# Local attention's score products: 64x64 tiles of the array, with unseen cells written once a stage

## The reference, cut to what matters

```python
W, H, DH = 64, 8, 64                       # window, heads, width of a head
qkv = x @ Wqkv.T                           # x: layer-normed, 8 x 256 x 128
# q, k, v -> (batch, head, window, 64, 64); ke, ve: the window before, its own, the one after
sim = jnp.einsum('bhnid,bhnjd->bhnij', q, ke) * SCALE
sim = jnp.where(valid[None, None, :, None, :], sim, -1000000000.0)   # no window before the first, after the last
attn = jax.nn.softmax(sim, axis=-1)
o = jnp.einsum('bhnij,bhnjd->bhnid', attn, ve)
...
return o @ Wout.T
```

## Time and profile before

| | us |
|---|---|
| median of three launches | 1091.48 |
| the profiled launch | 1089.49 |
| its span | 1087.7 |
| first routed stage, light branch (about 317 to 503) | 186 |
| second routed stage, light branch (about 800 to 986) | 186 |
| TensorE busy in the span | 966.8 |
| VectorE busy in the span | 670.0 |
| ScalarE busy in the span | 381.5 |

### The profile page before, as it was taken

One profiled execution on the slowest core, in us unless ns is written; L12 is line 12 of the kernel. 1 busy time (PEld: TensorE's weight loads), 2 busy tenths in 40 slices (PEclk: granted clock), 3 DMA queues, 4 the chain that ended last, 5 costly groups with the idle time before them and its releaser, 6 DMA issues.

```text
span 1087.7 us, 23083 instructions
## 1 busy us (share of the span) xinstructions
PE 966.8 (89%) x8840; PEld 698.3 (64%) x8840; DVE 670.0 (62%) x1914; ACT 381.5 (35%) x913; POOL 141.6 (13%) x289
## 2 busy tenths in 40 slices
PE   3499999899559999999999589999879999999997
PEld 3378888788446666667776245555446667667775
DVE  5778787887664565566555456667453665565553
ACT  3321111111333434333332136667623433333332
POOL 5011111110110000000000254350010000000000
PEclk9889898999689999999999569999979999999997
DMA  5000000000000000000000233322000000000000
GB/s 188 0 2 1 2 0 0 0 0 1 0 1 1 1 2 2 2 2 2 1 0 1 60 86 97 82 75 75 3 1 1 2 1 2 2 2 2 10 10 20
DMA packets 13751, 20.07 MB, mean 18 GB/s; under 512 B 1504, under 2 KB 12128, under 8 KB 12256
## 3 DMA queue, kind: packets, MB, share of 16 engines
q1 hardware_dynamic: 13520, 18.67, 5.9%
q10 hardware_dynamic: 144, 0.20, 0.1%
HBM read 14.53 MB, written 4.19 MB: 17 GB/s over the span
## 4 chain that ended last, share of the span: by engine, by line
PE 70%; DVE 13%; issue 10%; ACT 4%; POOL 2%; DVEq 1%; DMA 1%; SPq 0%; POOLq 0%; ACTq 0%
PE bank L1598 6%; PE bank L1659 6%; PE bank L1627 6%; PE bank L1645 5%; PE bank L1685 3%; PE bank L1605 3%; PE bank L604 3%; PE bank L1083 2%; PE bank L1833 2%; PE bank L1828 2%; PE bank L589 2%; PE bank L1104 2%; PE bank L1631 2%; PE bank L1117 2%; PE bank L1803 2%
## 5 line engine op out<-in xcount | busy, mean ns | idle before, releaser
L1398 DVE TENSOR_REDUCE arena<-bank 128x2 f32<-128x512 f32 x128 | 85.0, 688 | 53.3 <-PE bank L1083 52.2
L2166 DVE TENSOR_REDUCE arena<-bank 128x4 f32<-128x768 f32 x64 | 61.3, 958 | 65.6 <-PE bank L1631 65.6
L1221 ACT ACTIVATE arena<-bank 128x512 f32<-128x512 f32 x128 | 74.5, 594 | 51.0 <-PE bank L1104 50.2
L604 PE MATMUL bank<-arena 128*128 128x9 f32 x512 | 66.2, 257 | 13.4 <-DVE arena L929 7.5
L604 PEld LDWEIGHTS bank<-arena 128*128 128x128 f32 x512 | 65.6, 200 | 16.6 <-issue 8.7
L1627 PE MATMUL bank<-arena 64*128 64x192 f32 x512 | 76.2, 374 | 0.0
L1598 PE MATMUL bank<-arena,w_sb 128*128 128x256 f32 x256 | 74.5, 418 | 1.3 <-ACT arena L1924 1.3
L589 PE MATMUL bank<-arena 128*128 128x128 f32 x512 | 72.1, 289 | 0.3 <-DVE arena L863 0.3
L1945 ACT ACTIVATE arena<-bank 128x768 f32<-128x768 f32 x64 | 51.9, 811 | 55.8 <-PE bank L1649 54.1
L589 PEld LDWEIGHTS bank<-arena 128*128 128x128 f32 x512 | 67.1, 203 | 2.8 <-DVE arena L863 0.3
L1645 PE MATMUL bank<-arena 64*128 64x192 f32 x512 | 66.2, 356 | 0.4 <-ACT arena L1945 0.4
(11 more groups left out here) (297 smaller groups left out, 1978.4 us busy)
## 6 DMA issues: line engine op xcount, KB each, us to landing
arena<-q_dram SPq DMA_DIRECT2D x24, 192.0 KB
arena<-k_dram SPq DMA_DIRECT2D x24, 192.0 KB
w_sb<-w_dram SPq DMA_DIRECT2D x2, 1578.5 KB, 11.0
q_dram<-arena SPq DMA_DIRECT2D x24, 64.0 KB, 2.9
k_dram<-arena SPq DMA_DIRECT2D x24, 64.0 KB, 2.1
x<-x_dram SPq DMA_DIRECT2D x4, 256.0 KB, 4.4
out_dram<-x SPq DMA_DIRECT2D x4, 256.0 KB, 2.3
c_sb<-c_dram SPq DMA_DIRECT2D x1, 601.5 KB, 6.5
```

The costliest lines, as they stand in the source:

```text
L604: ins = pe.matmul(bank[7][:, h * 144 + k * LV:h * 144 + (k + 1) * LV], l_a[:, u % 2, j, :], l_v[parity][:, h * LH + k, :], start=u == 0 an ...
L1221: act.activation(a_pT[:, u % (2 * GROUP), :, :].rearrange("p k t -> p (k t)"), bank[2 + u % 2][:, :], ACT.Exp).then_inc(S["p"], 1)
L1398: dve.tensor_reduce(a_mx[:, i % 2, :, u % GROUP], bank[s % 2][:, :].rearrange("p (h k) -> p h k", h=HALVES), AX_X, ALU.max, negate=True).t ...
L2166: dve.tensor_reduce(g_mx[:, s, :, :, i].rearrange("p h j -> p j h"), two_banks(0)[:, :, 0:SPAN].rearrange("p j (h k) -> p j h k", h=HALVES ...
```

## The change

- `scores` goes over the four windows instead of the halves. `window(n)` gives the 64 partitions that the window's rows go to (n odd: the upper 64), the columns in the bank, and the keys that it sees: 128 for the windows 0 and 3, 192 for 1 and 2. Windows are taken in the pairs (0, 3) and (2, 1), so that the two of a pair write different partitions. With j = 0, 1 that makes four 64x64 products with different rows or columns of the array. L1631's products are gone.
- `turned_scores` does the same with k and q exchanged: for each pair of windows the four bf16 products with `marks` come first, then the four fp32 ones.
- The cells that no window sees are no longer written by TensorE. VectorE writes -1e9 there once a stage (`close_windows(0)` and `close_windows(2)`, four instructions in all), since nothing else writes them before the stage's light branch is through.
- `g_row`, `g_neg` and 9 of GpSimd's 16 fills go; `marks` shrinks from 256 to 64 columns of the table of constants, so that the load of the constants has 98 KB less.
- TensorE's order changes: `scores(b+1, p)` now stands directly behind `turned_scores(b, p)` in all four slots, ahead of the projection. In slot 0 `turn_tops` comes ahead of `project_qk("q23")` and in the table `INPUTS` as well.

```diff
-        marks = c("marks").bitcast(BF16).rearrange("p (i k c) -> p i k c", i=2, k=HALVES)
+        marks = c("marks").bitcast(BF16).rearrange("p (i c) -> p i c", i=2)
...
-            for kind, of in (("q23", b + 1), ("m1", b), ("k23", b + 1), ("z", b + 2), ("v0", b + 1),
+            for kind, of in (("m1", b), ("q23", b + 1), ("k23", b + 1), ("z", b + 2), ("v0", b + 1),
...
+        WINDOW_PAIRS = ((0, 3), (2, 1))
+
+        def window(n):
+            first, last = max(n - 1, 0) * WIN, min(n + 2, T // WIN) * WIN
+            h = n // 2
+            shift = h * KEYS - h * WIN
+            return slice((n % 2) * WIN, (n % 2 + 1) * WIN), slice(first + shift, last + shift), slice(first, last)
...
-                for h in range(HALVES):
-                    for j in range(2):
-                        rows = slice(j * DH, (j + 1) * DH)
-                        pe.matmul(bank[j][:, h * KEYS:(h + 1) * KEYS], q[rows, pair, h * P:(h + 1) * P],
-                                  k[rows, pair, h * WIN:h * WIN + KEYS], start=True, stop=False, skip_group_check=True)
-                    far = h * KEYS + (KEYS - WIN if h == 0 else 0)
-                    for j in range(2):
-                        ins = pe.matmul(bank[j][:, far:far + WIN], g_row[j * DH:j * DH + 1, h, :],
-                                        g_neg[j * DH:j * DH + 1, :], start=False, stop=True, skip_group_check=True)
+                for windows in WINDOW_PAIRS:
+                    for n in windows:
+                        for j in range(2):
+                            at, cols, seen = window(n)
+                            rows = slice(j * DH, (j + 1) * DH)
+                            ins = pe.matmul(bank[j][at, cols], q[rows, pair, n * WIN:(n + 1) * WIN], k[rows, pair, seen],
+                                            start=True, stop=True, skip_group_check=True)
...
+                for windows in WINDOW_PAIRS:
+                    for n in windows:
+                        for j in range(2):
+                            at, cols, seen = window(n)
+                            rows = slice(j * DH, (j + 1) * DH)
+                            pe.matmul(bank[2 + j][at, cols], marks[rows, i, :], g_mT[s][rows, seen],
+                                      start=True, stop=False, skip_group_check=True)
+                    for n in windows:
+                        for j in range(2):
+                            at, cols, seen = window(n)
+                            rows = slice(j * DH, (j + 1) * DH)
+                            ins = pe.matmul(bank[2 + j][at, cols], k[rows, pair, n * WIN:(n + 1) * WIN], q[rows, pair, seen],
+                                            start=False, stop=True, skip_group_check=True)
...
                 if now:
                     turned_scores(b, 0)
                 if ahead:
-                    project_qk("q23", b + 1)
+                    scores(b + 1, 0)
                 if now:
                     turn_tops(b, 1)
                 if ahead:
-                    scores(b + 1, 0)
+                    project_qk("q23", b + 1)
...
+            def close_windows(i):
+
+                for n in range(2):
+                    at = slice(n * WIN, (n + 1) * WIN)
+                    dve.tensor_scalar(two_banks(i)[at, :, P + n * WIN:P + (n + 1) * WIN],
+                                      c("ones")[at, 0:2 * WIN].rearrange("p (j c) -> p j c", j=2), -BIG, None, ALU.mult)
+
...
             scale_z(0)
+            close_windows(0)
+            close_windows(2)
             normalise_group(1)
             copy_q("q01", 0)
```

More of the change, by code:

```diff
@@ L56 @@
           ("headrows", D), ("upto", P // SEG), ("count", 1), ("logk", 1), ("start", 1), ("is_q", 1), ("is_kv", 1),
-          ("share", 1), ("marks", 2 * HALVES * P // 2)]
+          ("share", 1), ("marks", WIN)]
 def columns(table):
@@ L104, in make_constants @@
     put("share", 1.0 / np.minimum(picks * FETCH, float(T)))
-    marks = np.zeros((P, 2, HALVES, P), np.uint16)
+    marks = np.zeros((P, 2, WIN), np.uint16)
     for j in range(2):
@@ L108, in make_constants @@
             marks[j * DH + 2 * i:j * DH + 2 * i + 2, i] = 0x3F80
-        marks[j * DH + 4, :, 0, 0:WIN] = 0x3F80
-        marks[j * DH + 5, :, 1, WIN:P] = 0x3F80
     put("marks", marks.reshape(P, -1).view(np.float32))
@@ L1459, in build @@
         GROUPS = 4
-        FILLS = 16
+        FILLS = 7
         SETS = PAIRS // 2
@@ L1721, in route_tensor @@
                 if ahead:
+                    scores(b + 1, 1)
                     project_qk("k23", b + 1)
@@ L1724, in route_tensor @@
                     turn_z(b + 2)
-                if ahead:
-                    scores(b + 1, 1)
                 if behind:
@@ L1737, in route_tensor @@
                     turned_scores(b, 2)
+                if ahead:
+                    scores(b + 1, 2)
                 if ahead2:
@@ L1741, in route_tensor @@
                     turn_tops(b + 1, 0)
-                    scores(b + 1, 2)
                 if now:
@@ L1753, in route_tensor @@
                     turned_scores(b, 3)
+                if ahead:
+                    scores(b + 1, 3)
                 if ahead2:
                     project_qk("k01", b + 2)
-                if ahead:
-                    scores(b + 1, 3)
                 if behind:
@@ L2059, in route_gpsimd @@
             link, end = chain(pool, S["zero"], FILLS, S["nth"])
-            link(pool.memset(g_neg[:], -BIG))
-            link(pool.memset(g_row[:, 0:1, 0:WIN], 1.0))
-            link(pool.memset(g_row[:, 0:1, WIN:P], 0.0))
-            link(pool.memset(g_row[:, 1:2, 0:WIN], 0.0))
-            link(pool.memset(g_row[:, 1:2, WIN:P], 1.0))
             link(pool.memset(g_mb[:], 0.0))
-            for j in range(2):
-                link(pool.memset(g_mb[0:WIN, :, 1, j * DH + 4], -BIG))
-                link(pool.memset(g_mb[WIN:P, :, 0, j * DH + 5], -BIG))
             link(pool.tensor_copy(g_identb, ident))
```

2 lines of the change are left out of this document (removed).

## The result

The changed kernel took 1040.75 us (median of 4 launches, 1034.19 to 1049.43), the one before, run beside it, 1098.13 us. The ratio is 0.951, 95% interval 0.9365 to 0.9654: faster by 5%. It leaves out one launch of the kernel before, of 1154.73 us, which fell in a slower state of the chip; the median of 1098.13 us has it in. The forecast was 1043 us, from 1031 to 1064. The profiled launch is the slowest of the four, 1049.43 us with a span of 1047.6.

A forecast was written before the change was run, and what follows sets the result against it. TensorE, busy throughout each routed batch, was taken as the bound. Gains of 55.4 and 1.8 us less 5.8, 3.6 and 1.6 make 46.2 us, from the profiled 1089.5 to 1043 us, range 1031 to 1064.

The forecast's parts named there:

- rival of the paced slot: Routed slots: top or the exponentials end late by 0.4 us in each of 56 slots, giving 1065 us; chance 0.13.
- The pair of scores: Turned scores plus scores in a slot: 2.36 to 1.37 us, gaining 0.99 us in each of 56 slots, 55.4 us.
- rival of two 64x64 products at once: Scores and turned scores: a pair's windows run one behind the other, 2.55 us a slot, 1107 us in all; chance 0.05.
- Loads: Slot's ten groups of four: 64-column loads not hidden behind matmuls on the same rows, 28 us, 1071 us; chance 0.03.
- keeps its 1.06 us: Projection in each slot: price unchanged at 1.06 us, since it still stands between blocks of other tile shapes.
- (1): Start of each routed stage: waits for maxima and copies make first turned scores 2.9 us later, 5.8 us in both stages.
- (2): Scores(b+1, 1) waits for the maximum behind copy_q(q23): 0.3 us a batch, 6 batches a stage, 3.6 us lost.
- (3): Batch 0, which has no values yet: v0 waits some 0.8 us for k23's copy, 1.6 us lost in all.
- What costs nothing: VectorE's four close_windows, at most 0.24 us each, hidden by a 2.55 us wait; GpSimd's fills off the path; constants 0.
- The sum: Whole kernel: 55.4 + 1.8 - 5.8 - 3.6 - 1.6 = 46.2 us gained.

The follow-up runs named there:

- the last experiment: The change with the old order at the start, but 64x128 products two at once, without one-row products, instead of 64x64 four at once: 1054.23 us, ratio 0.959.
- the maximum first: The change with VectorE's top(b+1, 0) moved ahead of copy_q(q23) and scale_z: 1032.09 us, ratio 0.945 to the kernel before.

## Why the prediction was right, point by point

**The bound.** TensorE filled the batches before and fills them now. Products taken off it came off the time, with no other engine in the way. The rival of the paced slot falls: the batch shown has no wait of TensorE.

**The pair of scores.** Forecast 2.36 to 1.37 us, 0.99 a slot; measured 2.37 to 1.36, 1.01. Four products at once, the unproved step, is shown by the rows of slot 3; the last experiment prices the tiles. So the rival of two 64x64 products at once falls. No kernel was made that forces them into twos, so its 1107 us wasn't measured.

**Loads.** The rival falls. 64-column loads run beside matmuls on the same rows:

```profile
863.34 0.49 PE L1656 MATMUL bank<-arena 64*64 64x192 f32 x8
863.51 0.52 PEld L1634 LDWEIGHTS bank<-arena 64*64 64x64 f32 x16
...
863.67 0.71 PE L1634 MATMUL bank<-arena 64*64 64x128 f32 x16
```

L1634's loads start 0.16 us ahead of its matmuls, while L1656 streams. The Trainium skill (TensorE: Matmul & The Clock Gate, Part 3: Packing small matmuls, The mechanism) says that a load overlaps a running matmul only when the row group differs. In these rows both row groups are busy (L1656 has products of j = 0 and j = 1) and the loads overlap all the same, so the measurement decides. The same section also names a background weight buffer into which a load may be pulled ahead, which would fit; no run here tests it.

**The projection "keeps its 1.06 us".** Wrong in slot 3: there it now stands next to project_out, which has its shape, so that it takes 0.97 and not 1.06 us, and project_out 0.89 and not 1.00: 0.2 us together. The 1.06 us was the price of slot 3 alone from the start. Slots 0, 1 and 2 gained 1.06, 1.01 and 1.01 us, slot 3 1.21. That is 3 us over both stages that the sum lacks (0.2 us in six slots of a stage, and 0.05 in slot 0).

**(1) The start.** Forecast 14.9 us, measured 14.44 and 17.22. The mechanism is right: the two waits for the maximum and the one for k23's copy stand in the rows. Against the 2.9 us a stage forecast it cost 2.5 us in the second stage and 5.2 in the first, there with a clock that I had not put in. Against what was to be had (9.65) it cost 4.8 and 7.6.

**(2) A wait of 0.3 us a batch.** Wrong: there is none. VectorE after the projection in slot 0:

```profile
865.56 0.69 DVE L2156 TENSOR_SCALAR arena<-bank 128x512 f32<-128x512 f32 x1 [0.59 <-PE bank L1603]
866.17 0.47 DVE L2150 TENSOR_SCALAR arena<-y_all,scales 128x128 f32<-128x128 f32 x2
866.56 0.95 DVE L2164 TENSOR_REDUCE arena<-bank 128x4 f32<-128x768 f32 x1
```

The chain was put at 3.42 us and TensorE's own work at 3.11; both came to 3.18, from the projection's start at 864.44 to the scores' at 867.62. The copy starts 1.12 us after the projection and not 1.17. The maximum starts 1.00 us after the copy, not 1.08, and ends at 867.51; scores start 0.11 us later and not 0.21. My 0.21 came from a start at which TensorE stood idle; why it is less here no run shows. With the maximum first the batch stayed at 18.48, so it was even and not late. 3.6 us that the sum took off too much.

**(3) Batch 0** gained 23.43 - 19.53 = 3.90 us against 4.29 of a middle batch: 0.4 us a stage and not 0.8.

**What costs nothing.** `close_windows` takes 0.29 us for one (8 in the trace), and not at most 0.24 as bounded: 1.2 us a stage. VectorE waits 1.2 us behind it for the first projection, so it is hidden, with half of the cover left. The bound was wrong, which cost nothing.

**The sum.** 46.2 us forecast; 52.2 in the traces of the routed stages: 3 for slot 3, 3.6 for (2), 0.8 for (3), 1 for the pair, less 2 for the start (7.7 us in both stages and not 5.8, by the clock of the first). What is left is under 1 us. So the mechanism was right and its sum 6 us (13%) too small. That the result of 1040.75 lies only 2 us under the forecast is luck: one launch against another can be off by 10 us and more, as the 12 us ahead of and between the stages are here.

What made the gain, from the stages of these kernels: 30 us for leaving out the one-row products, 11 us for scores behind turned scores (163.0 to 157.4, in both stages), 23 us for the 64x64 tiles; and the change's own start gives 12 us of it back. They add up to the 52 us measured.

## What to carry to other kernels

Where TensorE is the bound, read the gaps between blocks of different tile shape first: here a product that does almost nothing cost as much as two changes of shape, and work of one shape put together saved one. Count the columns of products on different rows or columns once, and put neighbours on different ones. Small tiles pay where they leave work out. An order that pays in the steady loop is to be priced apart at the loop's ends, where buffers and queues are not yet filled.

## What the runs showed of the hardware that was not expected

- Four of the six starts with a wait of 2.04 us had a granted clock of 0.67 to 0.89, so that four records of 256 columns took 2.08 us and not 1.13. The other 18 starts had 0.98 or 1.00. Cause and effect weren't told apart.
- 64x64 fp32 products overlap across the border of two blocks that write different banks and different partitions, with start times 0.02 us apart.
- Loads of 64 columns ran beside matmuls on the same rows: they start 0.16 us ahead of their own matmuls and the blocks are no longer for it than their columns, a first load and an end.
- A change of tile shape costs 0.15 to 0.2 us (0.16 a pair between 64x64 and 128x128 tiles, 0.20 between the projection and project_out when scores stood between them), and a one-row product acts as a shape of its own: two in a half made it 0.23 us longer than without them.
